# The shared expert's third token chunk behind the routed works, with its weights loaded and split a second time

## The reference

```
h = patches @ W.T + b
h = h + attn0(layernorm(h))
h = h + ffn0(layernorm(h))      # 8 experts, top 2, and a shared expert, hidden 768
h = h + attn1(layernorm(h))     # its constants: log_tau = exp(clip(prior_log_tau, -50, 30))
h = h + ffn1(layernorm(h))      # 3 experts, top 2, and a shared expert, hidden 384

def expert(xf, W1, W2, W3):     # of ffn0
    gate = minimum(xf @ W1, 10)
    up = clip(xf @ W3, -10, 10)
    return silu(gate) * up @ W2

scores = sqrt(softplus(x @ gate_w)); indices = top_k(scores + gate_bias, 2)
weights = scores[indices] / clip(sum(scores[indices]), 1e-6)
ffn0 = expert(x, w1s, w2s, w3s) + sum over the 2 picks of weights * expert_e(x)
```

## Time and profile before

| | |
|---|---|
| median of three runs | 682.21 us (682.0 to 684.53) |
| span of the profiled execution | 682.5 us |
| busy: TensorE, VectorE, ScalarE, GpSimd | 561.2, 421.6, 248.8, 241.1 us |
| chain that ended last, share | TensorE 57%, VectorE 23%, issue 12%, ScalarE 4%, GpSimd 2%, DMA 1% |
| moved by DMA | 62.80 MB, mean 92 GB/s |
| transfers of `stage` for ffn0 | 17 of 1536 KB |
| transfers of `w0d` | 17 of 576 KB, 3.9 us to landing |

### The profile page before, as it was taken

The page is one execution under the profiler, slowest core; times in us unless marked ns, Lnnn a source line. Parts: engine busy times, 40 slices in busy tenths (PEclk is TensorE's granted clock), DMA queues, the critical chain, the costliest instruction groups (busy, mean ns, idle before and its releaser), DMA issues.

```text
span 682.5 us, 10313 instructions
## 1 busy us (share of the span) xinstructions
PE 561.2 (82%) x3648; PEld 536.3 (79%) x3648; DVE 421.6 (62%) x882; ACT 248.8 (36%) x509; POOL 241.1 (35%) x182
## 2 busy tenths in 40 slices
PE   5797488948899999999999156668889868999997
PEld 6676487938798988988999146557879858999997
DVE  0626747625588788788785267787585554445554
ACT  1323433104353453453451122543544323334431
POOL 1300400360365465465461555275463410002200
PEclk9978777978999999999999668968787868899999
DMA  9800000351645654664632222000010100000001
GB/s 344 335 0 1 1 0 1 110 214 31 235 141 169 235 217 165 228 221 165 222 136 69 65 59 121 1 0 1 1 63 3 44 21 1 0 1 1 1 1 54
DMA packets 23624, 62.80 MB, mean 92 GB/s; under 512 B 6336, under 2 KB 16480, under 8 KB 20896
## 3 DMA queue, kind: packets, MB, share of 16 engines
q1 hardware_dynamic: 17504, 55.59, 22.7%
q0 software_dynamic: 1728, 3.54, 1.6%
q10 hardware_dynamic: 4352, 3.15, 1.4%
HBM read 53.32 MB, written 8.95 MB: 91 GB/s over the span
## 4 chain that ended last, share of the span: by engine, by line
PE 57%; DVE 23%; issue 12%; ACT 4%; POOL 2%; DMA 1%; DVEq 0%; SPq 0%; ACTq 0%
PE bank L584 16%; PE bank L402 9%; PE bank L418 5%; DVE a0h L686 4%; PE bank L931 4%; DVE a0t L682 4%; PE bank L602 3%; PE bank L945 3%; PE bank L736 2%; PE bank L903 2%; PE bank L757 2%; PE bank L805 2%; POOL G L1277 2%; DVE Y L1381 1%; DVE XWl L694 1%
## 5 line engine op out<-in xcount | busy, mean ns | idle before, releaser
L686 DVE SCALAR_TENSOR_TENSOR a0h<-a0s,a0t 128x256 f32<-128x256 f32 (+1 forms) x114 | 114.3, 1002 | 13.5 <-ACT a0s L654 1.0
L644 POOL TENSOR_TENSOR w0l<-stage,w0h 128x768 fp32r<-128x768 f32 x32 | 58.6, 1831 | 146.1 <-ACT w0h L628 125.8
L654 ACT ACTIVATE a0s<-bank 128x256 f32<-128x256 f32 (+1 forms) x114 | 45.5, 400 | 153.1 <-PE bank L584 126.8
L602 PE MATMUL bank<-w0d,a0h 128*128 128x192 f32 x492 | 83.6, 328 | 1.0 <-DVE H L703 1.0
L602 PEld LDWEIGHTS bank<-w0d,a0h 128*128 128x128 f32 x492 | 80.4, 191 | 1.3 <-DVE H L703 1.3
L682 DVE TENSOR_SCALAR a0t<-bank 128x256 f32<-128x256 f32 (+1 forms) x114 | 50.2, 440 | 50.2 <-PE bank L584 40.9
L584 PE MATMUL bank<-XWh,w0h 128*128 128x256 f32 x192 | 56.8, 296 | 13.8 <-DVE XWl L694 8.7
L642 POOL TENSOR_TENSOR w0t<-stage,w0t 64x768 fp32r<-64x768 f32 x32 | 58.3, 1821 | 4.6
L584 PE MATMUL bank<-XWh,w0t 128*128 128x256 f32 x192 | 54.3, 283 | 0.0
L584 PE MATMUL bank<-XWh,w0l 128*128 128x256 f32 x192 | 54.2, 282 | 0.0
L584 PE MATMUL bank<-XWl,w0t 128*128 128x256 f32 x192 | 54.2, 282 | 0.0
(11 more groups left out here) (255 smaller groups left out, 1444.6 us busy)
## 6 DMA issues: line engine op xcount, KB each, us to landing
stage<-moe0w SPq DMA_DIRECT2D x17, 1536.0 KB
w0d<-moe0d SPq DMA_DIRECT2D x17, 576.0 KB, 3.9
stage<-moe1w SPq DMA_DIRECT2D x4, 1056.0 KB, 5.0
patch<-patches SPq DMA_DIRECT2D x4, 768.0 KB, 8.0
slots_in<-zero SPq DMA_DIRECT2D x4, 768.0 KB, 16.7
XR<-slots_in SPq DMA_DIRECT2D x16, 192.0 KB, 3.8
slots_out<-YO ACTq DMA_DIRECT2D x16, 192.0 KB, 2.0
XR<-slots_in SPq DMA_DIRECT2D x16, 64.0 KB, 3.7
```

What stands on the lines that cost most here:

```text
L602: last = nc.tensor.matmul(bank[e_bank(qpar, t, shared)][:, 0:D], A0["h"][qpar][:, fc, t * P:(t + 1) * P], W0[par]["down"][:, fc, :], start ...
L644: ins = engine.tensor_tensor(W0[par]["l"][:, mat, :], src, W0[par]["h"][:, mat, :].bitcast(F32), ALU.subtract)
L654: nc.scalar.activation(A0["s"][fc % 2][:, 0:width], bank[fc % 2][:, 0:width], ACT.Silu).then_inc(S0["silu_ready"], 1)
L686: nc.vector.scalar_tensor_tensor(out=A0["h"][qpar][:, fc, 0:width], in0=A0["s"][fc % 2][:, 0:width], scalar=SILU_LIMIT, in1=A0["t"][fc % 2 ...
```

## The change

Chunk 2 of the shared expert goes behind the works. Its six units and its down projection leave the front on TensorE, ScalarE and VectorE. Its weights, which are the same for all chunks, have been overwritten by then, so SyncE loads them a second time into the buffers of parity 1 (1.5 MB and 576 KB), ScalarE converts them between the SiLUs of work 16, as it does for a next work, and GpSimd splits them behind its sixteenth. On TensorE the last order is: gate-and-up of work 16, down of work 15, units 0 and 1 of chunk 2, down of work 16, units 2 to 5 of chunk 2, its down. ScalarE stores work 15 behind the SiLU of chunk 2's unit 0 and work 16 behind that of unit 2. VectorE copies work 16 behind unit 1 and adds chunk 2 last. All counts in the waits move by the three downs and six units that no longer come first. The outputs are those of the reference as before. The diff, its context cut:

```diff
@@ -344,7 +344,7 @@
                 if n >= 2:
-                    sp.wait_ge(S["down_ready"], 9 + 2 * (n - 2))
+                    sp.wait_ge(S["down_ready"], 6 + 2 * (n - 2))
                 sp.dma_start(W0[n % 2]["down"].rearrange("p a b -> p (a b)"), moe0d[bass.ds(
@@ -367,6 +367,10 @@
                 load_down(n)
+            sp.wait_ge(S["w_lo"], 4 * WORKS)
+            sp.dma_start(W0[1]["stage"][:], moe0w[0]).then_inc(ld_stage[1], 16)
+            sp.wait_ge(S["down_ready"], 6 + 2 * (WORKS - 1))
+            sp.dma_start(W0[1]["down"].rearrange("p a b -> p (a b)"), moe0d[0]).then_inc(ld_w2[1], 16)
             sp.wait_ge(ln_var, 3 * CH)
@@ -591,11 +595,13 @@
                 if shared:
-                    d = 3 * q + t
-                    if d >= 2:
+                    d = 3 * min(q, 2) + t
+                    if q == WORKS + 2 and t < 2:
+                        pe.wait_ge(y_done, 2 * WORKS)
+                    elif d >= 2:
                         pe.wait_ge(S0["acc_done"], d - 1)
                 elif isinstance(n, int) and n == 1:
-                    pe.wait_ge(S0["acc_done"], 8 + t)
+                    pe.wait_ge(S0["acc_done"], 6)
                 else:
@@ -698,9 +704,10 @@
 
+            par, first = (1, 6 + 2 * WORKS) if c == 2 else (c, 3 * c)
             for t in range(3):
-                dve.wait_ge(S0["down_ready"], 3 * c + t + 1)
-                nc.vector.tensor_tensor(H[:, 3 * c + t, :], bank[e_bank(c % 2, t, True)][:, 0:D], H[:, 3 * c + t, :],
+                dve.wait_ge(S0["down_ready"], first + t + 1)
+                nc.vector.tensor_tensor(H[:, 3 * c + t, :], bank[e_bank(par, t, True)][:, 0:D], H[:, 3 * c + t, :],
                                         ALU.add).then_inc(S0["acc_done"], 1)
@@ -708,7 +715,7 @@
             for t in range(WT // P):
-                dve.wait_ge(S0["down_ready"], n * 2 + (8 + t))
+                dve.wait_ge(S0["down_ready"], n * 2 + (5 + t))
                 nc.vector.tensor_copy(YO[par][:, t, :], bank[e_bank(0, t, False)][:, 0:D]).then_inc(y_done, 1)
@@ -823,18 +830,16 @@
             e_down(pe, 0, 0, 0, 0, True, 16)
-            e_gate_up(pe, 2, 0, 0, 2)
             e_down(pe, 1, 1, 0, 0, True, 16)
-            e_down(pe, 2, 0, 0, 0, True, 16)
             e_rows(pe, 1, 1, 32)
...
 
-                e_gate_up(pe, n + 2, n, par, None)
+                e_gate_up(pe, n + 1, n, par, None)
                 if not last:
...
                 if w2_loaded is not None:
-                    e_down(pe, n + 1, 1 - par, n - 1, 1 - par, False, w2_loaded)
+                    e_down(pe, n, 1 - par, n - 1, 1 - par, False, w2_loaded)
 
@@ -846,7 +851,11 @@
             e_pe(WORKS, 0, None, 8 * WORKS, last=True)
-            e_down(pe, WORKS + 2, 0, WORKS, 0, False, 8 * WORKS + 16)
+            tail = WORKS + 2
+            e_gate_up(pe, tail, WORKS + 1, 1, 2, range(2))
+            e_down(pe, WORKS + 1, 0, WORKS, 0, False, 8 * WORKS + 16)
+            e_gate_up(pe, tail, WORKS + 1, 1, 2, range(2, FC0))
+            e_down(pe, tail, 1, WORKS + 1, 1, True, 8 * WORKS + 16)
 
@@ -1077,27 +1086,26 @@
             e_act(act, 1, CHW, None, None, None)
-            e_act(act, 2, CHW, None, None, None)
             for n in (1, 2):
...
 
-            e_act(act, 3, WT, None, (2, 0, None), None)
-            e_act(act, 4, WT, (3, 1, 48, 4), (3, 1, 24), None)
-            e_act(act, 5, WT, (4, 0, 64, 5), (4, 0, 30), (1, 1))
-            e_act(act, 6, WT, (5, 1, 64, 6), (5, 1, 36), (2, 0))
+            e_act(act, 2, WT, None, (2, 0, None), None)
+            e_act(act, 3, WT, (3, 1, 48, 3), (3, 1, 18), None)
+            e_act(act, 4, WT, (4, 0, 64, 4), (4, 0, 24), (1, 1))
+            e_act(act, 5, WT, (5, 1, 64, 5), (5, 1, 30), (2, 0))
             with act.Fori(0, (WORKS - 6) // 2, 1) as i:
-                e_act(act, i * 2 + 7, WT, (i * 2 + 6, 0, i * 16 + 80, i * 2 + 7), (i * 2 + 6, 0, i * 12 + 42),
+                e_act(act, i * 2 + 6, WT, (i * 2 + 6, 0, i * 16 + 80, i * 2 + 6), (i * 2 + 6, 0, i * 12 + 36),
                       (i * 2 + 3, 1))
-                e_act(act, i * 2 + 8, WT, (i * 2 + 7, 1, i * 16 + 80, i * 2 + 8), (i * 2 + 7, 1, i * 12 + 48),
+                e_act(act, i * 2 + 7, WT, (i * 2 + 7, 1, i * 16 + 80, i * 2 + 7), (i * 2 + 7, 1, i * 12 + 42),
                       (i * 2 + 4, 0))
-            e_act(act, WORKS + 1, WT, (WORKS, 0, 8 * WORKS + 32, WORKS + 1), (WORKS, 0, FC0 * (WORKS + 1)),
+            e_act(act, WORKS, WT, (WORKS, 0, 8 * WORKS + 32, WORKS), (WORKS, 0, FC0 * WORKS),
                   (WORKS - 3, 1))
-            e_act(act, WORKS + 2, WT, None, None, (WORKS - 2, 0))
-            e_store(act, WORKS - 1, 1)
-            e_store(act, WORKS, 0)
+            e_act(act, WORKS + 1, WT, (WORKS + 1, 1, 8 * WORKS + 32, WORKS + 1), None, (WORKS - 2, 0))
+            e_act(act, WORKS + 2, CHW, None, None, None,
+                  {0: lambda: e_store(act, WORKS - 1, 1), 2: lambda: e_store(act, WORKS, 0)})
             act.wait_ge(l1_tau, 1)
@@ -1269,6 +1277,7 @@
             e_split_low(nc.gpsimd, pool, WORKS, 0)
+            e_split_low(nc.gpsimd, pool, WORKS + 1, 1)
 
@@ -1605,21 +1614,23 @@
                   {2: bases, 3: slots, 4: experts})
-            e_dve(dve, 2, 0, CHW, 3, None, lambda: e_acc(dve, 1), {0: lambda: share(sc, E0, comb[:], True), 1: weights})
+            e_acc(dve, 1)
             e_split_low(nc.vector, dve, 1, 1)
-            e_acc(dve, 2)
+            share(sc, E0, comb[:], True)
+            weights()
             dve.wait_ge(x_hi, 1)
             nc.vector.tensor_tensor(XWl[1][:], bank[6][:], XWh[1][:].bitcast(F32), ALU.subtract).then_inc(x_lo, 1)
-            e_dve(dve, 3, 1, WT, 6, (2, 0), None)
-            e_dve(dve, 4, 0, WT, 9, (3, 1), lambda: e_copy(dve, 1, 1, None))
-            e_dve(dve, 5, 1, WT, 11, (4, 0), lambda: e_copy(dve, 2, 0, None))
-            e_dve(dve, 6, 0, WT, 13, (5, 1), lambda: e_copy(dve, 3, 1, 16))
+            e_dve(dve, 2, 1, WT, 6, (2, 0), None)
+            e_dve(dve, 3, 0, WT, 6, (3, 1), lambda: e_copy(dve, 1, 1, None))
+            e_dve(dve, 4, 1, WT, 8, (4, 0), lambda: e_copy(dve, 2, 0, None))
+            e_dve(dve, 5, 0, WT, 10, (5, 1), lambda: e_copy(dve, 3, 1, 16))
             with dve.Fori(0, (WORKS - 6) // 2, 1) as i:
-                e_dve(dve, i * 2 + 7, 1, WT, i * 4 + 15, (i * 2 + 6, 0), lambda: e_copy(dve, i * 2 + 4, 0, i * 16 + 16))
-                e_dve(dve, i * 2 + 8, 0, WT, i * 4 + 17, (i * 2 + 7, 1), lambda: e_copy(dve, i * 2 + 5, 1, i * 16 + 32))
-            e_dve(dve, WORKS + 1, 1, WT, 2 * WORKS + 3, (WORKS, 0), lambda: e_copy(dve, WORKS - 2, 0, 8 * WORKS - 32))
-            e_dve(dve, WORKS + 2, 0, WT, 2 * WORKS + 5, None, lambda: e_copy(dve, WORKS - 1, 1, 8 * WORKS - 16))
-            e_copy(dve, WORKS, 0, 8 * WORKS - 16)
+                e_dve(dve, i * 2 + 6, 1, WT, i * 4 + 12, (i * 2 + 6, 0), lambda: e_copy(dve, i * 2 + 4, 0, i * 16 + 16))
+                e_dve(dve, i * 2 + 7, 0, WT, i * 4 + 14, (i * 2 + 7, 1), lambda: e_copy(dve, i * 2 + 5, 1, i * 16 + 32))
+            e_dve(dve, WORKS, 1, WT, 2 * WORKS, (WORKS, 0), lambda: e_copy(dve, WORKS - 2, 0, 8 * WORKS - 32))
+            e_dve(dve, WORKS + 1, 0, WT, 2 * WORKS + 2, None, lambda: e_copy(dve, WORKS - 1, 1, 8 * WORKS - 16))
+            e_dve(dve, WORKS + 2, 1, CHW, 2 * WORKS + 4, None, lambda: e_acc(dve, 2),
+                  {1: lambda: e_copy(dve, WORKS, 0, 8 * WORKS - 16)})
 
...
             nc.vector.tensor_scalar(tau[:], row[0:GW, R_TAU:R_TAU + HEADS], -50.0, 30.0, ALU.max,

```

## The result

The changed kernel took 692.74 us, the median of four runs (689.96 to 694.87), beside 683.37 us (682.0 to 684.92, four runs) for the kernel before: a ratio of 1.0122, 95% interval 1.0096 to 1.0148. It is slower, by 8 to 9 us. The time lies inside the range, but the forecast was "no change", so the prediction was wrong in its likeliest case.

The account below looks back on a forecast made before the run. It took chunk 2, not the scatters, to bound the chain in front of the routed works. 682.5 - 14.25 (front) + 12.7 (end) + 0.9 (late reports) = 681.85, less 0.3 gave 681.5 us, no change; range 676 to 695.5.

Parts of the forecast that it names:

- The base: Whole kernel before: a span of 682.5 us, 0.3 us above the median of its three runs, 682.21.
- rival 3: In front: chunk 2's hole is only the profiler's, so the change gives 696.8 us, slower; chance 0.18.
- Front, the rows: Before the routed works: work 1's rows land at 155.4, allowing the first routed matmul at 157.4.
- Front, VectorE's chain: Before the routed works: late report at 149.5, then addition, splits 4.1, routing operations 2.7, row split: 157.4.
- Front, clock: First routed work: TensorE's idling from 139 to 155 lowers its clock and costs 1.9 us, between 0 and 3.8.
- End, late weights: Last round: chunk 2's weights land at 369.9 and block ScalarE's first conversion for 4.9 us.
- End, order of TensorE: Two chunk 2 units before work 16's down cost 3.5 us; gather starts at 390.85, last down ends at 400.4.
- End, the scales: Before the first mixture: layer 1's scale constants, formerly hidden under the gather, put 2.9 us on the path.
- End, late reports: During the gather: one late report falling on chunk 2 adds 0.9 us, between 0 and 1.8.
- Rival 1: Last round: the weights' transfer doesn't hold ScalarE, the end costs 7.8 us, giving 676.6; chance 0.10.
- Rival 2: In front: chunk 1's last down is reported at 154.0, VectorE's chain gives 162.0, total 686 us; chance 0.11.
- Rival 4: At the end: the hole moves beside the 18 gathers, 14.3 us more, 696 us; chance 0.15.

Follow-up runs that it names:

- r2: Changed kernel with the shared weights' second load put ahead of work 16's down weights on SyncE: 677.17 us, ratio 1.0118 to the kernel before.
- r0: The changed kernel, unedited, run again on a quiet chip: 681.57 us beside 670.17 for the kernel before, ratio 1.0175.
- r4: The kernel before, unchanged, one run on a quiet chip: 668.14 us.
- r11: The kernel before without GpSimd's 18 indirect scatters, one run on a late chip: 669.76 us beside 684.07.
- r13: Changed kernel, late chip: weights' load, down(16), stores, first scale operation, routing and splits earlier; third tile's chunk 2 addition behind first mixture: 683.01 us, before 683.02.
- r10: The kernel before with VectorE's splits of work 1 regrouped between chunk 1's additions, rows transposed earlier, on a late chip: 681.02 us, ratio 0.9963.
- r14: The kernel before with the weights' loads of works 1 and 2 held until the scatters are done, one run, late chip: 681.56 us, before 683.02.
- r9: Changed kernel with VectorE's last routing operations made to wait for GpSimd's first split of work 2: 686.59 us, ratio 1.0247 to the kernel before.

## Why the prediction was wrong, point by point

- **The base.** I took the 682.5 us span as 0.3 us above the time. In all runs of the kernel before whose spans are on record, the time is 1.6 to 1.7 us above the run's own span (1.8 to 1.9 for the changed kernel, 689.96 and 688.1), so the execution of the earlier trace rows took about 684.1 us and was one of the slower ones. The 9 to 15 us of launch work that rival 3 took from the Trainium skill ("Runtime: NRT & Kernel Launch", "The ~15µs preamble/postamble breakdown") are not in the difference between this case's times and spans.
- **Front, the rows.** Taken 155.4, measured 155.26, where TensorE's wait for them ends. Right. (Rows 4 and 5 give 154.95 for the first of their two transfers; the second goes out 0.43 us later.)
- **Front, VectorE's chain: the step that failed first.** Late report 149.5, measured 148.8; splits 4.1, measured 4.1; ten routing operations 2.7, measured 8.2. I priced them from rows where GpSimd issued scatters, and moved them to where GpSimd splits; a product of VectorE beside a split stood in the same trace with 1.54 us instead of 0.43. Works at 162.24, not 157.5.
- **Front, clock.** 1.9 us expected, 0.8 us measured on the first chip (9.2 us from the first matmul to work 2's rows, 8.4 before), 2.0 on quiet ones. Front together: 10.6 us gained, not 14.25.
- **End, late weights.** The transfer's time was right: 7.2 us behind the round's start (7.7 expected), ScalarE idle for 4.16 us (4.9). r2 gives 4.4 us for it.
- **End, order of TensorE.** The gather starts 27.9 us behind the round's start (28.7 expected), the last down projection ends 38.3 us behind it (38.2). Both right.
- **End, the scales.** I put 2.9 us on the path; they took 1.5 us (394.9 to 396.39), since ScalarE had loaded its table at 383.04, while it waited. 1.4 us too much.
- **End, late reports: the second step that failed.** I allowed 0.9 us. The third tile's report was 4.6 us late and the second mixture waited 2.3 us more; on quiet chips both are nil. The end cost 18.0 us, not 13.6 (12.7 and the 0.9). On quiet chips it cost 13.6, and that agreement is luck: there nothing was late, the scales took 1.4 us less, and the last down projection ended 40.9 us behind the round's start (349.24 to 390.14 in r0) instead of 38.2, with the lower clock behind the late weights.
- **The rivals.** Rival 1 is out. Rival 2 is out in its cause (the report was no later than I took), though its start of 162.0 came true. Rival 3 asked the right question, whether the hole is there, and priced the case without it at 1.9 + 12.7 us. On quiet chips the hole is not there, and the change costs 11.4 us in the runs and 14.6 between the traces of r4 and r0; the trace of r4 is of one of the shortest runs. That the profiler makes it isn't shown: r11 shows the scatters do, on a late chip. Whether an execution that nobody records has late reports there is open, as every run here is recorded. Rival 4 came true in part, with 4.6 us here and 12.0 in r13.
- **What I should have seen.** Chunk 2 ran beside the scatters, whose rows landed at 155.4; without the hole it would have ended at 155.3 by rival 3's own sum. Nearly the whole gain that I took was the hole and what followed it, a wait that no instruction of the kernel accounts for.

## What to carry to other kernels

Chunk 2 lay beside a transfer that the next stage waited for, and cost next to nothing there; moving it away could gain only the unexplained hole. Run the kernel before on a second chip before building on such a hole. Price a moved operation by rows with the same neighbour: small VectorE operations took 0.23 us alone and up to 1.8 us beside a GpSimd split. Where an engine's result banks are fewer than its tiles, an addition that is put off holds the engine.

## What the runs showed of the hardware

- TensorE's reports of completion come late on some chips while GpSimd's indirect scatters run: by 10.7 us for chunk 1's last down on the first chip (ended near 138.1, heard at 148.8), in r10 and r14 with waits of 4 to 8 us; and by 4.6 us (12.0 in r13) beside the indirect gathers. Without the scatters they are on time (r11). On other chips, with the same kernel, they are on time (r4). For the kernel before that is 670 or 683 us. They are not TensorE's alone: at the end of the gathers VectorE's waits for its own operations took 1.76 us (404.20, kernel before) and 2.26 us (405.12, changed kernel) on the first chip, and in the nine traces of changed kernels and the one of the kernel before from quiet chips VectorE has no wait of 0.9 us or more whose end the profile can't put down to an instruction or a transfer.
- VectorE's TENSOR_TENSOR on 72 elements and TENSOR_SCALAR on 9, all operands in SBUF, last until the GpSimd TENSOR_TENSOR that runs at the time ends (r9: 1.4 to 1.7 us, alone 0.23); a reduce of that size does not (0.23), nor a clip of 128x256 that reads a bank (0.41 at 361.80 on the first chip, beside a split from 361.74).
- The same instructions behind the projections took 279.1 to 282.5 us in the seventeen traces, with a granted clock of 0.74 to 0.83 between 460 and 520 us; no run tells what sets it.
